# Attention's opening in a fused attention and soft-expert kernel: x loaded and turned by halves of tokens, and half of the first query head rotated by GpSimd

## The reference, cut to what matters

```python
q = (x @ Wq) ; k = (x @ Wk) ; v = (x @ Wv)          # by heads of 128
def rotate_half(t):
    t1, t2 = jnp.split(t, 2, axis=-1)
    return jnp.concatenate((-t2, t1), axis=-1)
q = q * cos + rotate_half(q) * sin                  # and k alike
scores = einsum('bhid,bhjd->bhij', q, k) * scale    # causal mask, softmax
out = einsum('bhij,bhjd->bhid', softmax(scores), v) * head_scale
```

## Time and profile before

| | us |
|---|---|
| median of 3 runs | 1204.24 (1203.88 to 1205.72) |
| the profiled execution, its own time | 1204.42 |
| its span, first to last instruction | 1202.6 |
| TensorE busy | 1139.5 (95%) |
| VectorE, ScalarE, GpSimd busy | 804.0, 791.9, 712.2 |

### The profile page before, as it was taken

One profiled execution on the slowest core, in us unless ns is written; L12 is line 12 of the kernel. 1 busy time (PEld: TensorE's weight loads), 2 busy tenths in 40 slices (PEclk: granted clock), 3 DMA queues, 4 the chain that ended last, 5 costly groups with the idle time before them and its releaser, 6 DMA issues. The chain is left out here.

```text
span 1202.6 us, 23558 instructions
## 1 busy us (share of the span) xinstructions
PE 1139.5 (95%) x8096; PEld 1048.5 (87%) x8096; DVE 804.0 (67%) x1899; ACT 791.9 (66%) x1654; POOL 712.2 (59%) x485
## 2 busy tenths in 40 slices
PE   5899999999999999999999999999999999999977
PEld 4799999999998998899999999998778888898866
DVE  4575676666677568667676766776676575777767
ACT  2566766666675666678776766664477795567654
POOL 2677667667774765678676675530276654565521
PEclk9899999999999999999999999999999999999989
DMA  3231121111211112111111111200101101010011
GB/s 101 71 123 45 36 53 45 32 28 50 58 28 32 45 32 58 39 37 28 49 37 48 32 45 36 49 7 19 36 23 27 28 18 32 19 28 19 10 44 36
DMA packets 48789, 47.57 MB, mean 40 GB/s; under 512 B 13080, under 2 KB 43288, under 8 KB 48416
## 3 DMA queue, kind: packets, MB, share of 16 engines
q1 hardware_dynamic: 48384, 45.99, 14.8%
q10 hardware_dynamic: 288, 0.07, 0.0%
HBM read 24.03 MB, written 2.10 MB: 22 GB/s over the span
## 5 line engine op out<-in xcount | busy, mean ns | idle before, releaser
L536 PE MATMUL ring<-kT,qT 128*128 128x384 f32 (+5 forms) x1152 | 244.2, 347 | 3.1 <-ACT exps L701 2.6
L701 ACT ACTIVATE exps<-ring,neg_max 128x128 f32<-128x128 f32 (+7 forms) x256 | 189.3, 742 | 55.9 <-DVE neg_max L845 55.0
L845 DVE CUSTOM_DVE_ANT_0 ring<-ring,hidden 128x128 f32<-128x128 f32 (+7 forms) x256 | 191.6, 769 | 22.0 <-PE ring L536 21.1
L718 ACT ACTIVATE exp_parts<-turned 128x512 fp32r<-128x512 f32 x192 | 114.6, 597 | 133.9 <-PE turned L551 113.6
L536 PEld LDWEIGHTS ring<-kT,qT 128*128 128x128 f32 x1152 | 186.0, 189 | 14.3 <-issue 3.7
L572 PE MATMUL mix<-exp_parts,v_parts 128*128 128x256 f32 x1152 | 184.5, 296 | 0.4 <-DVE exp_parts L863 0.4
L551 PE MATMUL turned<-ident,exps 128*128 128x128 f32 x1152 | 178.5, 273 | 4.5 <-DVE exp_parts L863 3.8
L551 PEld LDWEIGHTS turned<-ident,exps 128*128 128x128 f32 x1152 | 141.3, 141 | 22.8 <-issue 3.6
L863 DVE TENSOR_TENSOR exp_parts<-turned,exp_parts 128x512 fp32r<-128x512 f32 x192 | 131.9, 687 | 29.3 <-ACT exp_parts L718 29.1
L572 PEld LDWEIGHTS mix<-exp_parts,v_parts 128*128 128x128 f32 x1152 | 149.4, 190 | 0.6 <-DVE exp_parts L863 0.6
L973 POOL TENSOR_TENSOR cos_part<-taken,cos_sb 128x1024 f32<-128x1024 f32 x38 | 91.3, 2402 | 94.7 <-ACT taken L669 94.7
(11 more groups left out here) (225 smaller groups left out, 2185.1 us busy)
## 6 DMA issues: line engine op xcount, KB each, us to landing
rotated<-taken SPq DMA_DIRECT2D x76, 256.0 KB, 3.7
raw_q<-in_L_attn_Wq_dram SPq DMA_DIRECT2D x32, 128.0 KB, 3.6
raw_o<-in_L_attn_Wo_dram SPq DMA_DIRECT2D x32, 128.0 KB, 3.3
ffn_mu_next<-in_L_ffn_mu_dram SPq DMA_DIRECT2D x28, 128.0 KB, 2.4
y_sb<-in_L_attn_x_dram SPq DMA_DIRECT2D x2, 1024.0 KB, 7.4
exps_and_mu<-in_L_ffn_mu_dram SPq DMA_DIRECT2D x1, 2048.0 KB, 9.6
ffn_w_sb<-in_L_ffn_W_dram SPq DMA_DIRECT2D x8, 256.0 KB
ffn_w_sb<-in_L_ffn_W_dram SPq DMA_DIRECT2D x14, 128.0 KB, 2.6
```

What stands on the lines that cost most here:

```text
L536: last = nc.tensor.matmul(ring_cols(item, half * BANK, piece), qT[:, H % QUERIES, a, i * P:(i + 1) * P], kT[:, G % 2, m, half * piece:(hal ...
L701: nc.scalar.activation(dst, tile, ACT.Exp, bias=neg_max[:, H % 2, i:i + 1], scale=-1.0, accum_out=row_sum[:, H % 2, i:i + 1]).then_inc(don ...
L718: nc.scalar.activation(exp_parts[:, slot % HELD, 0, :], turned[:, n % 2, :], ACT.Copy).then_inc(done[kind], 1)
L845: nc.vector.tensor_tensor_reduce(tile, tile, later, -1.0, 3.0e38, ALU.add, ALU.min, neg_max[:, H % 2, i:i + 1]).then_inc(done[kind], 1)
```

## The change

- **x by halves of tokens.** x of sequence 0 comes in two DMAs of 512 KB, the first ahead of the weights of k and q, the second behind them. The tables come as four DMAs, by the same halves. Sequence 1 is loaded in two DMAs too.
- **Both halves turned first, split by depth.** A step turns 4 token tiles for both feature halves. For sequence 0 it writes into `turned` (half 0) and `mix` (half 1) in place of the ring, and its split is made in two pieces of 512 columns, one for each feature half. A `first` projection waits for the feature half that it is about to use, and only for its own half of tokens.
- **One half of q by GpSimd.** The second half of tokens of query head 0 is projected right behind k 0, taken out by ScalarE, and rotated by GpSimd in the way of the later heads (512 columns each). VectorE rotates three pieces in place of four. The order becomes k 0, q 1, q 0, k 1, v on TensorE; on VectorE all three pieces come before the first two score blocks; on ScalarE `rope_hi` of that half stands ahead of `take` of v.
- **Identity turned while x travels.** TensorE makes 22 transposes of the identity, whose results nobody reads, before it waits for x.
- In the expert layer three names for a square root become one kind, `std`, with the same waits; a semaphore that nobody waited for is gone.

The diff, cut to its core:

```diff
-    def turn_x(b, c):
-        plan.extend([("turn_x", b, c), ("xT_hi", b, c), ("xT_lo", b, c)])
+    def turn_x(b, half):
+        plan.append(("turn_x", b, half))
+        for which in ([(b, half, 0), (b, half, 1)] if b == 0 else [(b, half)]):
+            plan.extend([("xT_hi", *which), ("xT_lo", *which)])
 
     weights("k", 0)
     weights("q", 0)
-    plan.append(("load_tables",))
+    plan.extend([("load_x", 0, 1), ("load_tables", 0), ("load_rest", 1)])
     weights("v", 0)
     weights("q", 1)
+    def piece(who, half):
+        plan.extend([(kind, who, half) for kind in ("near", "far", "join", "part_hi")])
+
     turn_x(0, 0)
     turn_x(0, 1)
-    def pieces(half):
-        for who in ("k", "q"):
-            plan.extend([(kind, who, half) for kind in ("near", "far", "join", "part_hi")])
-        plan.extend([("part_lo", who, half) for who in ("k", "q")])
-
-    plan.extend([("first", "k", 0), ("first", "q", 0), ("project", "v", 0), ("first", "k", 1), ("first", "q", 1)])
-    pieces(0)
-    plan.append(("take", "v", 0))
+    plan.extend([("first", "k", 0), ("first", "q", 1), ("take", "q", 0), ("swap", "q", 0)])
+    piece("k", 0)
+    plan.extend([("first", "q", 0), ("first", "k", 1), ("project", "v", 0)])
+    piece("q", 0)
+    plan.extend([("part_lo", "k", 0), ("part_lo", "q", 0)])
+    plan.extend([("times_cos", "q", 0), ("times_sin", "q", 0), ("rope_add", "q", 0)])
+    piece("k", 1)
+    plan.extend([("rope_hi", "q", 0), ("rope_lo", "q", 0), ("take", "v", 0)])
+    plan.append(("part_lo", "k", 1))
     for i in range(2):
         plan.extend([("scores", 0, i), ("max", 0, i), ("exp", 0, i)])
-    pieces(1)
     plan.append(("turn_v", 0))
     rope("q", 1)
...
+        def rope_cols(who, n):
+            return slice(BANK if (who, n) == ("q", 0) else 0, N)
+        def x_turned(b, half, c):
+            return ring_cols(("turn_x", b, half), c * BANK, BANK) if b else (turned, mix)[half][:, c, :]
...
+            def idle_products(n):
+                for _ in range(n):
+                    nc.tensor.transpose(mix[:, 1, 0:P], ident[:, :], ident[:, :])
+            idle_products(22)
...
                 if kind == "turn_x":
-                    for t in range(TILES):
-                        last = nc.tensor.transpose(ring_cols(item, t * P, P), y_sb[:, b * TILES + t, c * P:(c + 1) * P], ident[:, :])
+                    for c in range(KT):
+                        for t in range(TILES // 2):
+                            last = nc.tensor.transpose(x_turned(b, half, c)[:, t * P:(t + 1) * P],
+                                                       y_sb[:, b * TILES + half * TILES // 2 + t, c * P:(c + 1) * P], ident[:, :])
...
                 if kind == "first":
-                    pe.wait_ge(done["xT_lo"], count("xT_lo", 0, KT - 1))
                     for k, (c, a, m) in enumerate(passes):
+                        if (a, m) == PARTS[0]:
+                            pe.wait_ge(done["xT_lo"], count("xT_lo", 0, half, c))
...
                 if kind == "scores":
-                    if H == 0:
-                        pe.wait_ge(done["part_lo"], count("part_lo", "q", i // 4))
+                    if H == 0 and i < 4:
+                        pe.wait_ge(done["part_lo"], count("part_lo", "q", 0))
+                    elif H == 0:
+                        pe.wait_ge(done["part_lo"], count("part_lo", "k", 1))
+                        pe.wait_ge(done["rope_lo"], count("rope_lo", "q", 0))
...
                 if kind == "take":
+                    if (who, n) == ("q", 0):
+                        act.wait_ge(done["first"], count("first", "q", 1))
+                        nc.scalar.activation(taken[:, BANK:N], ring_cols(("first", "q", 1), 0, BANK), ACT.Copy).then_inc(done[kind], 1)
+                        continue
...
                 if kind == "times_cos":
-                    nc.gpsimd.tensor_tensor(part, taken[:, :], cos_sb[:, :], ALU.mult).then_inc(done[kind], 1)
+                    nc.gpsimd.tensor_tensor(part, taken[:, cols], cos_sb[:, cols], ALU.mult).then_inc(done[kind], 1)
```

More of the change, by code:

```diff
@@ L157, in plan_attention @@
         if H == 0 and n == 2 and sequences > 1:
-            plan.append(("load_x", 1))
+            plan.extend([("load_x", 1, half) for half in range(2)])
         plan.append(("turn_exps", H, w, p))
@@ L338, in ring_cols, with xT_count @@
             return ring[:, lo:lo + width]
+        def x_turned(b, half, c):
+            return ring_cols(("turn_x", b, half), c * BANK, BANK) if b else (turned, mix)[half][:, c, :]
+        def xT_count(kind, b, half):
+            return count(kind, b, half) if b else count(kind, b, half, KT - 1)
         def sequence(who, n):
@@ L414, in _ @@
                         sp.wait_ge(done["rope_add"], count(kind, *which) - 1)
[L415 to L418, removed]
+                    if count(kind, *which) == 2:
+                        sp.wait_ge(done["join"], 3)
+                    cols = rope_cols(*which)
+                    sp.dma_start(rotated[0:64, cols], taken[64:128, cols]).then_inc(done[kind], 16)
+                    sp.dma_start(rotated[64:128, cols], taken[0:64, cols]).then_inc(done[kind], 16)
                 if kind == "load_o":
@@ L442, in free_ring @@
                     if kind == "turn_x":
-                        pe.wait_ge(done["xT_lo"], count("xT_lo", *which))
+                        pe.wait_ge(done["xT_lo"], xT_count("xT_lo", *which))
                     if kind == "first":
-                        pe.wait_ge(done["far"], count("far", *which))
+                        if which == ["q", 1]:
+                            pe.wait_ge(done["take"], count("take", "q", 0))
+                        else:
+                            pe.wait_ge(done["far"], count("far", *which))
                     if kind == "project":
@@ L504, in _ @@
                     pe.wait_ge(done["weights_lo"], count("weights_lo", who, n))
[L505 removed]
+                    pe.wait_ge(done["xT_lo"], xT_count("xT_lo", b, 1))
                     free_ring(item)
@@ L1003, in deviations @@
     def deviations(b):
-        put(*[(kind, b) for kind in ("vary", "std_1", "inv_1", "std_2", "inv_2", "offsets")])
+        put(("vary", b), ("std", b, "rows"), ("inv_1", b), ("std", b, "twice"), ("inv_2", b), ("offsets", b))
     def output(v):
@@ L1618, in _ @@
                                          turned_at_item(("turn", g, half)).rearrange("p (t s) -> p t s", s=S), ACT.Copy).then_inc(done[kind], 1)
-                if kind in ("std_1", "std_2"):
-                    (b,) = which
-                    before = "vary" if kind == "std_1" else "inv_1"
-                    act.wait_ge(done[before], count(before, b))
-                    nc.scalar.activation(std[:, b, :], spread_sq[:, b, :], ACT.Sqrt).then_inc(done[kind], 1)
-                if kind == "std_3":
-                    b, part = which
-                    act.wait_ge(done["vary_3"], count("vary_3", b, part))
-                    ts = tiles_of(b, part)
+                if kind == "std":
+                    b, part = which
+                    ts = slice(0, TILES) if part in ("rows", "twice") else tiles_of(b, part)
+                    if part == "rows":
+                        act.wait_ge(done["vary"], count("vary", b))
+                    elif part == "twice":
+                        act.wait_ge(done["inv_1"], count("inv_1", b))
+                    else:
+                        act.wait_ge(done["vary_3"], count("vary_3", b, part))
                     nc.scalar.activation(std[:, b, ts], spread_sq[:, b, ts], ACT.Sqrt).then_inc(done[kind], 1)
@@ L1768, in _ @@
                     (b,) = which
-                    dve.wait_ge(done["std_1"], 1)
+                    dve.wait_ge(done["std"], count("std", b, "rows"))
                     step(nc.vector.reciprocal(inv_1[:, b, :], std[:, b, :]))
@@ L1778, in _ @@
                     (b,) = which
-                    dve.wait_ge(done["std_2"], 1)
+                    dve.wait_ge(done["std"], count("std", b, "twice"))
                     nc.vector.reciprocal(inv_2[:, b, :], std[:, b, :]).then_inc(done[kind], 1)
@@ L1955, in _ @@
                     means = mean_var[:, b, ts, 0:1].rearrange("p t a -> p (t a)")
-                    dve.wait_ge(done["std_3"], count("std_3", b, part))
+                    dve.wait_ge(done["std"], count("std", b, part))
                     step(nc.vector.reciprocal(inv_1[:, b, ts], std[:, b, ts]))
```

92 lines of the change are left out of this document (57 added, 35 removed).

## The result

| us | before | after |
|---|---|---|
| median (range, runs), same chip | 1204.06 (1203.38 to 1205.72, 4) | 1195.34 (1194.87 to 1196.58, 4) |
| profiled execution, its own time | 1204.42 | 1195.39 |
| its span | 1202.6 | 1193.6 |

The ratio is 0.993 with a 95% interval of 0.9917 to 0.9944: the change makes the kernel faster, by 8.7 us in the medians and 9.0 in the two profiled executions, where 4.6 were forecast.

A forecast was written before the change was run, and what follows sets the result against it. TensorE sets the pace from 57 us, so only the opening's chain (x, VectorE's pieces, turning of v, GpSimd) can gain: earlier first piece 5.0, shorter chain 2.1, meetings -2.5, sum 4.6; forecast 1199.6 us, range 1197.0 to 1202.0.

The forecast's parts named there:

- x half 1 in at 9.9: Opening: the second half of x lands at 9.9 us, when the query weights landed before.
- late x: Rival, opening: x's second half lands with the last load, 12.4; 2.5 us less, gain 2.1, 1202.1 us; chance 0.06.
- The full clock for the 8 turns: Opening, TensorE: after 6.8 us of unbroken work, x's second half is turned at full clock in 1.04 us.
- Half clock at x: Rival, opening: idle turns do not raise TensorE's clock in time; 1.4 us less, gain 3.2, 1201.0 us; chance 0.12.
- Meetings with GpSimd of 2.5 us: Opening: VectorE's two-SBUF-input steps wait for GpSimd's products of q, costing 2.5 us; none to 3.6 possible.
- no meeting: Rival, opening: the swap lands late or GpSimd slips between VectorE's steps; gain 7.1 us, 1197.1 us; chance 0.18.
- v turned at about 28: Opening, TensorE: v is turned at about 28 us, where it was 32.64 before.
- The low part of v at 32.2: Opening, GpSimd: its low part of v comes at about 32.2 us, where it was 36.81 before.
- Cover for `rope_hi`: Opening: GpSimd's sum of q ends near 22.2, ScalarE wants it at 26.4; hidden, with 4 us of cover.
- Slower: Rival, opening: GpSimd's rotation delays ScalarE's take of v if the swap lands after 28.6; at 17 us, 1207.4; chance 0.04.
- Everything behind it is as it was.: Behind the turning of v: all stays as before, only 4.6 us earlier, so the gain is that turning's shift.
- given back: Rival, heads: their pattern is held by something that does not move with the opening; 1204 us; chance 0.08.

## Why the prediction missed

The direction was right, and the opening came near: 5.2 us over all traces, 4.6 forecast. That the profiled pair shows just 4.6 is luck. The total was wrong by 4.3 us. Step by step:

- **x half 1 in at 9.9.** It landed at 2.73 + 7.4 = 10.1, 0.2 later than forecast, and not at 12.4: *late x* is refuted. All of x was in 0.9 us later than by the one load (9.2). The prediction's "No row here shows a half-size load" overlooks the sine table, a load of 512 KB in 8.6 us. The Trainium skill, "DMA: Bandwidth & Descriptors", section "Bandwidth", advises batching loads to 1 MiB and more. For two loads of 512 KB in place of one of 1 MB this trace shows a price of at most those 0.9 us, with two loads of weights between them.
- **The full clock for the 8 turns.** 1.09 us against 1.04 forecast; 1.97 without the idle turns. *Half clock at x* is refuted. First piece at 13.15 against 13.2.
- **Meetings with GpSimd of 2.5 us.** Above 0.69, the two `join` and the first `part_lo` cost 0.50, 0.53 and 1.06: 2.1 us. The first `join` was held by GpSimd's weights, which ended at 16.00 in place of 15.5; the sine product and the sum each came one VectorE step earlier than named, at the second `join` and at the first `part_lo`. GpSimd's own products, forecast at 1.2, took 1.75, 1.29 and 1.53, and 1.27 to 1.30 where they met nothing. The Trainium skill, "SBUF — State Buffer", section "Who interferes with whom", is borne out by these rows; *no meeting* is refuted.
- **v turned at about 28.** 27.23. That is 0.4 us less of meetings and 0.4 less elsewhere in the chain.
- **The low part of v at 32.2.** 31.39, 5.4 us earlier in place of 4.6; GpSimd's wait of 0.81 for a swap at 40.40, not forecast and in this trace alone, brings it back to 4.6. The 0.8 us by which v came earlier than forecast were hidden by it.
- **Cover for `rope_hi`.** The sum of q ends at 19.49 + 1.53 = 21.02, and `rope_hi` starts at 25.56: 4.5 us of cover, 4 forecast. *Slower* had no ground.
- **"Everything behind it is as it was."** This is the step that failed. It was drawn from one stretch of 22.65 us behind the opening and applied to 1145 us, and *given back* was argued from the same stretch ("no idle time after 57 us"). TensorE is idle for 43.5 us behind 57 us in the kernel before. There the old kernel had a pause of TensorE of 1.70 us, with a fall of the clock behind it, that hung on 0.09 us between VectorE and GpSimd. A shift of the opening isn't handed on unchanged past such a place. In the profiled pair this place gave 3.3 us and the second one 1.5. The range allowed for meetings in the opening alone, and *given back* for the wrong sign.

By the move of `mu_inv` in the old kernel and the traces that passed, the first 3 to 4 us are shown as to cause: the wait that the prediction had priced for the opening acts there on a step of 16 elements. Two things stay open: why the swap ahead of it lands some tenths later in some executions of the changed kernel, and how often it does (two of four traces). The medians of the changed kernel hang on that share. To force or to forbid the meeting in the changed kernel with nothing else moved was not tried. The fall near 490 is chance by the traces, and no run here says what decides it.

## What to carry to other kernels

A forecast that hands a shift on to the end needs a look at every pause of the bounding engine along the whole span, and for each the distance in time by which its cause was met: a short step that takes ten times its own duration is such a place, and can be mended by itself (here one number gave 4.2 us). Work that is shared out to an engine that contends with the one it relieves is worth what remains after the meetings and the steps that come in with it, here 0.2 us of the 2.8 that one piece of VectorE takes (four steps of 0.69). Where executions spread more after a change than before, look for a race between two engines that tenths of a us decide.

## What the runs showed of the hardware

- A step of VectorE of 16 elements a partition takes 0.23 us alone and 2.31 to 2.32 when it starts 0.09 us behind a GpSimd product of 2.38 us. The length of the wait is that of GpSimd's instruction, not of its own.
- The wait goes both ways: GpSimd's product of 1.27 to 1.30 us took 1.75 and 1.53 where a VectorE step with two SBUF inputs lay across it.
- The pair of swap DMAs, of the same bytes each time, took 3.93 to 4.62 us at one and the same place of the list over seven traces of the two kernels, from the second issue to the product that waits for it.
- At one and the same pause of 1.95 us the granted clock fell to half in twelve traces and stayed full in one. It fell behind each of five pauses of 1.65 to 1.80 us, and did not behind one of 2.33 (at 47.55 in the first trace of after), so the length of a pause alone does not decide.
